# A fifth table-multiplied tile in a product-key memory kernel: head 4's last tile goes through its whole table instead of being gathered

## Chip, cores and metric

The kernel runs on one core of a Trainium2 chip. The metric is the device time of one execution in microseconds (us), smaller being better; the median of three runs is taken. The five engines of the core (TensorE or PE, VectorE or DVE, ScalarE or ACT, GpSimd or POOL, SyncE or SP) run their own instruction queues in order and wait for one another on semaphores.

## What is computed

For each of 16 batches of 512 tokens with 128 features there is a graph layer (layer norm, two products, a mean over neighbours, relu, residual) and then a memory layer with 8 heads. Per head and token, two lists of 128 scores give the 16 best each, the 256 sums give the 16 best pairs, and their softmax weighs 16 rows of keys and values out of a table of 16384 rows. Causal attention over the 512 tokens follows.

```python
q = (x @ Wq).reshape(b, n, HEADS, DIM) * DIM ** (-0.5)
kv_scores, indices = _pk(x, Wq_pk, pk_keys)          # 16 of 16384 rows per head and token
ind = indices + offsets[None, None, :, None]
k = jnp.einsum('bnhk,bnhkd->bnhd', kv_scores, keys_table[ind])
v = jnp.einsum('bnhk,bnhkd->bnhd', kv_scores, values_table[ind])
sim = jnp.einsum('bihd,bjhd->bhij', q, k)
sim = jnp.where(causal, sim, neg)
attn = jax.nn.softmax(sim, axis=-1)
out = jnp.einsum('bhij,bjhd->bhid', attn, v)
return out.transpose(0, 2, 1, 3).reshape(b, n, HEADS * DIM) @ Wo
```

## The kernel before, in words

A batch has 512 tokens, T = 4 tiles of 128. Heads 0 to 6 (GH = 7) are **gathered**: the loop of a batch runs over 28 tiles n (head n // 4, tile n % 4). For each tile GpSimd issues 16 indirect DMAs (L391) that bring 128 rows of 1 KB each into one of three buffers `got`; before them it waits for the row numbers (`rows_ready`) and, since there are three buffers, for the combination that last read this buffer (`combined`). TensorE combines the rows with their weights in 32 instructions into `comb_ps` (L664), ScalarE scales them into `kv`, and attention follows: transposed keys (L544), scores (L548), `prob` transposed (L554), values (L560), the product with Wo (L566). After tiles 1 and 3 of a head TensorE moves the next head's chosen rows and weights onto partitions (`move`, L499), which VectorE has prepared (`one_hot`, `hot_rows`, `sum_rows`, `lift`); VectorE then writes `rows` and `spread` (`take_moved`). At tile 0 of a head TensorE makes the next head's key scores and queries (`front`, L463 and L467) before it combines.

Head 7 is not gathered but **multiplied with its whole table** (the "dense" work). A pass k does this for 2 of the 128 keys of one side and 2 tiles: ScalarE raises four 128x128 exponentials (`raise_`, L790), VectorE compares ranks with counts and multiplies (`weigh`, L1214), TensorE transposes the four results (`turn`, L509), ScalarE copies them out (`take_wideT`, L725), and TensorE multiplies them with four 128x256 pieces of the table, eight instructions in the trace, adding up in `dense_ps` (`multiply`, L523). The buffers `expo`, `wide` and `wideT` are double. There are 64 passes for tiles 0 and 1 and 64 for tiles 2 and 3, 128 a batch. SyncE loads the table in chunks of 8 keys (1 MB) into two buffers `tab`; a load waits for `dense_done` of the chunk that it overwrites, and TensorE waits for `tab_loaded` every 4 passes. Before a half can start, VectorE ranks its scores and builds "hits", which TensorE adds to counts and ranks in `comb_ps` (`add_hits`, L490): four sets a half, eight a batch, at the tiles that `HITS` names.

The passes are laid between the steps of the gathered tiles by hand. `MIDDLE` has a row of five numbers for each of the 28 tiles of batches 0 to 14, `ENDING` for those of the last batch; they say how many passes each engine does after the combination, after the transposed keys, after the scores, before and after the transposed `prob`:

```python
THREE = (1, 0, 1, 1, 0)
FOUR = (1, 0, 1, 1, 1)
FIVE = (1, 1, 1, 1, 1)
SIX = (2, 1, 1, 1, 1)
SEVEN = (2, 1, 1, 2, 1)
```

`MIDDLE` has 16, 18, 20, 19, 19, 18 and 18 passes in its seven heads; `ENDING` 16, 22, 23, 23, 22, 22 and none in the last head. The next batch's graph layer lies at tiles 8 to 20, head 7's attention at tiles 17, 18, 1 and 2 (`OWN`, `LEFT`). In the text a "move" is L499, "fronts" are the operations that write `front_ps`.

Of the kernel before, what the change touches and what calls it, by code (L numbers as in the profile page):

```python
# [8 lines left out]
AX = mybir.AxisListType  # L9

P = 128
# [17 lines left out]

HALF_PASSES = NKEYS // 2  # L30
PASSES = 2 * HALF_PASSES
CHUNK = 4
KEYS = 2 * CHUNK
CHUNKS = PASSES // CHUNK

# [5 lines left out]
SEVEN = (2, 1, 1, 2, 1)  # L41
NONE = (0, 0, 0, 0, 0)
MIDDLE = [
    FIVE, FOUR, FOUR, THREE,
    SIX, FOUR, FIVE, THREE,
    SIX, FIVE, FIVE, FOUR,
    SIX, FIVE, FIVE, THREE,
    SIX, FOUR, FIVE, FOUR,
    SIX, FOUR, FIVE, THREE,
    SIX, FIVE, FOUR, THREE]  # L50
ENDING = [
    FIVE, FOUR, FOUR, THREE,
    SEVEN, FIVE, SIX, FOUR,
    SEVEN, FIVE, SIX, FIVE,
    SEVEN, FIVE, SIX, FIVE,
    SIX, FIVE, SIX, FIVE,
    SEVEN, FIVE, SIX, FOUR,
    NONE, NONE, NONE, NONE]
# [7 lines left out]
PREP = {1: 0, 0: 20}  # L66
HITS = {1: {4: (0, 1), 8: (2, 3)}, 0: {24: (0, 1), 26: (2, 3)}}
# [13 lines left out]
PAIRS = [(0, 2), (2, 2)]  # L81
FIRST_TILES = [(0, 1), (1, 1), (2, 2)]
# [15 lines left out]
def got_no(n):  # L98

    return n % 3 if n < SLOTS - 1 else 1  # L100


def got_back(n):

    return next(d for d in range(1, 6) if got_no((n - d) % SLOTS) == got_no(n))
# [16 lines left out]
def program(nc, x, adj, w_msg, w_upd, bias, wqpk_t, keys_t, wq, table, dense, wo, out):  # L122
# [78 lines left out]
    sim_d = sb("sim_d", [P, T, SIDES * NKEYS])  # L201
# [10 lines left out]
    z_inv = sb("z_inv", [P, T])  # L212
# [3 lines left out]
    rank1 = sb("rank1", [P, T, NKEYS])  # L216
    shift1 = sb("shift1", [P, T, NKEYS])
# [71 lines left out]
    dense_done, kv_d_copied = sem("dense_done"), sem("kv_d_copied")  # L289
    keyT_d_ready, keyT_d_copied = sem("keyT_d_ready"), sem("keyT_d_copied")  # L290
# [25 lines left out]
    def _(sp):  # L316
# [12 lines left out]
        def load_chunk(b, c, first=False):  # L329

            if not (first and c < 2):
                sp.wait_ge(dense_done, b * PASSES + (c - 1) * CHUNK)
            k = (c % (CHUNKS // 2)) * KEYS
# [15 lines left out]
        def batch(b, first=False, last=False):  # L349
# [5 lines left out]
            for c in range(CHUNKS):  # L355
                if c == 5 and not first:
                    store(b - 1)
                load_chunk(b, c, first)
# [6 lines left out]
    def _(pool):  # L365
# [13 lines left out]
        def batch(b, first=False, last=False):  # L379
            for n in range(SLOTS):  # L380
                h, t = n // T, n % T
                slot = b * SLOTS + n
# [3 lines left out]
                if not (first and n < 3):  # L386
                    pool.wait_ge(combined, slot - (got_back(n) - 1))
# [12 lines left out]
    def _(pe):  # L400
# [39 lines left out]
        def front(b, h, first=False, last=False):  # L440

            f = b * GH + h
            if h == 0:
                pe.wait_ge(xnT_copied, b * 2 + 2)
                pe.wait_ge(sim_d_copied, b * 2 + 1)
# [4 lines left out]
            elif h == 2:  # L450
                pe.wait_ge(sim_d_copied, b * 2 + 2)
                if not first:
                    pe.wait_ge(added_d, b * 4)
            elif h == 3:
                pe.wait_ge(q_d_copied, b + 1)
# [984 lines left out]
```

## Time and profile before

| | us |
|---|---|
| median of 3 runs | 9090.88 (9089.48 to 9093.23) |
| the profiled execution's own time | 9084.84 |
| its span, first to last instruction | 9083.0 |
| PE busy | 7878.3 (87%) |
| PEld (weight loads, beside PE) busy | 6137.2 (68%) |
| DVE busy | 7108.3 (78%) |
| ACT busy | 4886.8 (54%) |
| POOL busy | 6820.4 (75%) |
| mean granted TensorE clock | 0.928 of full |

A busy share is an average over the span. GpSimd's issue gaps between gathers are not counted as busy. A granted clock of 1.00 is 2.4 GHz, of 0.50 is 1.2 GHz; the engine has these two levels, and a mean lies between. The ends of matmuls are modelled, so that neighbouring groups overlap.

### The profile page before, as it was taken

What the parts mean: (1) busy time and instruction counts of PE and PEld (TensorE: products, weight loads), DVE (VectorE), ACT (ScalarE), POOL (GpSimd) and SP (SyncE); (2) the same over time, 40 slices, a digit from 0 to 9 for tenths busy, and PEclk for the clock granted to TensorE, in tenths of its full rate; (3) what the DMA queues carried; (4) which work ended last, traced back from release to release, by engine and by line L of the source; (5) the groups of instructions that cost most, each with busy time, mean ns of one, the idle gap of its engine ahead of it and who ended that gap; (6) DMA issues with size and microseconds to landing.
All of it is one profiled execution on the core that took longest, in us unless ns stands there. A gap on an engine that the chain in (4) does not pass through costs nothing.

```text
span 9083.0 us, 179526 instructions
## 1 busy us (share of the span) xinstructions
PE 7878.3 (87%) x51232; PEld 6137.2 (68%) x51232; DVE 7108.3 (78%) x30205; ACT 4886.8 (54%) x14163; POOL 6820.4 (75%) x7177
## 2 busy tenths in 40 slices
PE   5988888888888888888888888898888888889898
PEld 4766667667666766766667666676766766667676
DVE  7787787777878778787787877878778787787875
ACT  3555555555555555555555555464555555555554
POOL 5777777777777777777777777777777777777777
PEclk7999999999999999999999999999999999999998
DMA  4555555555555555555555555555555555555554
GB/s 133 170 171 165 168 168 170 168 167 167 172 165 167 171 166 168 170 167 166 166 172 166 168 169 168 168 171 168 169 166 169 168 166 170 172 162 171 162 179 146
DMA packets 445970, 1516.75 MB, mean 167 GB/s; under 512 B 123760, under 2 KB 141552, under 8 KB 379248
## 3 DMA queue, kind: packets, MB, share of 16 engines
q0 software_dynamic: 344064, 939.98, 33.8%
q1 hardware_dynamic: 100848, 564.37, 17.1%
q8 instruction: 456, 7.47, 0.3%
q14 instruction: 602, 4.93, 0.2%
HBM read 1499.66 MB, written 4.19 MB: 166 GB/s over the span
## 4 chain that ended last, share of the span: by engine, by line
POOL 49%; issue 18%; PE 16%; DVE 15%; ACT 1%; DMA 1%; POOLq 0%; DVEq 0%; SPq 0%; ACTq 0%
POOL got L391 49%; PE dense_ps L523 6%; DVE wide L1214 4%; PE comb_ps L664 3%; DVE hits L1178 2%; DVE chosen L1109 2%; PE wideT_ps L509 2%; DVE onehot L1104 1%; PE front_ps L463 1%; DVE onehot L1097 1%; PE score_ps L499 1%; DMA got<-in_table,rows 1%; DVE lifted L1117 1%; PE score_ps L548 1%; PE front_ps L467 1%
## 5 line engine op out<-in xcount | busy, mean ns | idle before, releaser
L391 POOL DMA_INDIRECT got<-in_table,rows x7168 | 6818.5, 951 | 2245.6 <-issue 2168.4
L523 PE MATMUL dense_ps<-tab,wideT 128*128 128x256 f32 x16384 | 4030.5, 390 | 10.6 <-ACT kv_d L725 9.4
L523 PEld LDWEIGHTS dense_ps<-tab,wideT 128*128 128x128 f32 x16384 | 3053.3, 195 | 669.9 <-issue 265.1
L1214 DVE SCALAR_TENSOR_TENSOR wide<-const_ps,rank,expo 128x128 f32<-128x128 f32 x8192 | 2299.3, 343 | 1357.6 <-PE wideT_ps L509 1039.4
L790 ACT ACTIVATE expo<-sim_d,shift 128x128 f32<-128x128 f32 x8192 | 2598.9, 394 | 128.8 <-DVE wide L1214 127.9
L725 ACT ACTIVATE wideT<-wideT_ps 128x512 f32<-128x512 f32 x2048 | 1212.9, 592 | 676.6 <-PE wideT_ps L509 669.9
L509 PE MATMUL wideT_ps<-ident,wide 128*128 128x128 f32 x8192 | 1255.4, 276 | 265.7 <-ACT wideT L725 243.1
L509 PEld LDWEIGHTS wideT_ps<-ident,wide 128*128 128x128 f32 x8192 | 1023.3, 143 | 534.4 <-issue 286.3
L664 PE MATMUL comb_ps<-got,spread 128*32 128x256 f32 x14336 | 1031.5, 436 | 135.6 <-DMA got<-in_table,rows 107.8
L664 PEld LDWEIGHTS comb_ps<-got,spread 128*32 128x32 f32 x14336 | 469.6, 122 | 587.7 <-issue 245.1
L725 ACT ACTIVATE kv<-comb_ps,wsum 128x256 f32<-128x256 f32 x448 | 210.4, 470 | 909.3 <-PE comb_ps L664 909.1
L499 PE MATMUL score_ps<-group_of,lifted 128*128 128x16 f32 x1792 | 296.9, 300 | 395.2 <-DVE lifted L1117 395.2
L499 PEld LDWEIGHTS score_ps<-group_of,lifted 128*128 128x128 f32 x1792 | 274.3, 234 | 439.2 <-DVE lifted L1117 414.4
L1178 DVE TENSOR_SCALAR hits<-iota_f,top_f_d,put 128x128 bf16<-128x128 f32 x2048 | 555.6, 365 | 0.6 <-DVE count_sb L1200 0.2
L725 ACT ACTIVATE sim<-front_ps 128x512 f32<-128x512 f32 x224 | 133.8, 597 | 669.9 <-PE front_ps L463 666.6
L830 ACT ACTIVATE prob<-neg,neg_max 128x128 f32<-128x128 f32 x448 | 250.9, 560 | 450.9 <-DVE neg_max L1231 450.6
L548 PE MATMUL score_ps<-keyT,qT 128*128 128x512 f32 (+3 forms) x896 | 341.5, 463 | 78.8 <-ACT keyT L725 78.8
L1109 DVE TENSOR_REDUCE chosen<-onehot 128x32 f32<-128x1600 f32 (+1 forms) x225 | 406.1, 1805 | 2.8
L1097 DVE TENSOR_TENSOR onehot<-place,const_ps 128x1600 f32<-128x1600 uint32 (+1 forms) x225 | 406.9, 1808 | 0.0
L1104 DVE TENSOR_TENSOR onehot<-onehot,const_ps 128x1600 f32<-128x1600 f32 (+1 forms) x225 | 405.5, 1802 | 0.1
L463 PE MATMUL front_ps<-w_sim,x2nT 128*128 128x256 f32 x888 | 358.3, 574 | 28.7 <-issue 28.7
L560 PE MATMUL score_ps<-probT,kv 128*128 128x128 f32 x2240 | 335.8, 281 | 53.2 <-ACT probT L725 53.2
(167 smaller groups left out, 7386.0 us busy)
## 6 DMA issues: line engine op xcount, KB each, us to landing
tab<-in_dense SPq DMA_DIRECT2D x512, 1024.0 KB
got<-in_table,rows POOLq DMA_INDIRECT x7168, 2.7
adj_i<-in_adj SPq DMA_DIRECT2D x16, 1024.0 KB
x_in<-in_x SPq DMA_DIRECT2D x16, 256.0 KB, 6.4
out<-fin SPq DMA_DIRECT2D x16, 256.0 KB, 6.0
tab<-in_wqpk_t SPq DMA_DIRECT2D x1, 512.0 KB, 10.5
tab<-in_keys_t SPq DMA_DIRECT2D x1, 512.0 KB, 14.8
wq_sb<-in_wq SPq DMA_DIRECT2D x1, 512.0 KB, 13.5
```

The lines of the kernel that those rows point to most:

```text
L391: pool.indirect_dma_start(out=got[got_no(n)][:, g, :], out_offset=None, in_=table, in_offset=bass.IndirectOffsetOnAxis(ap=rows[:, t * GATH ...
L499: mm = pe.matmul(moved_ps[:, 2 * q + u, :], lifted[:, u, q, :, :].rearrange("p e r -> p (e r)"), group_of[:, :], start=True, stop=True)
L509: mm = pe.transpose(wideT_ps[:, q * P:(q + 1) * P], wide[k % 2][:, q, :], ident[:, :])
L523: mm = pe.matmul(dense_ps[:, v * 2 * D:(v + 1) * 2 * D], wideT[k % 2][:, (2 * u + v) * P:(2 * u + v + 1) * P], tab[(k // CHUNK) % 2][:, (2 ...
L664: mm = pe.matmul(comb_ps[j * BAND:(j + 1) * BAND, 0:2 * D], spread[:, t, g, :], got[got_no(n)][:, g, :], start=(c == 0), stop=(c == PER_BA ...
L725: return act.activation(dst, src, ACT.Copy, scale=scale)
L790: last = act.activation(expo[k % 2][:, 2 * u + v, :], sim_d[:, 2 * half + v, 0:NKEYS], ACT.Exp, bias=shift1[:, 2 * half + v, key:key + 1])
L1097: after(link(dve.tensor_tensor(onehot[:, 0:nt, :, :].rearrange("p t k c -> p (t k) c"), place[:, t0:t0 + nt, :].rearrange("p t k -> p (t k ...
L1104: after(link(dve.tensor_tensor(hot, hot, cand[:, 0:nt, 1, :].unsqueeze(2).broadcast_to([P, nt, TOPK, NCAND]), ALU.mult)))
L1109: link(dve.tensor_reduce(chosen[:, 0:nt, 0, :], onehot[:, 0:nt, :, :], AX.X, ALU.add))
L1178: last = dve.tensor_scalar(hits[g % 2][:, a, :], iota_f[:, :], top_f_d[:, u, side, a:a + 1], put[:, u, side, a:a + 1], ALU.is_equal, ALU.mult)
L1214: last = dve.scalar_tensor_tensor(wide[k % 2][:, 2 * u + v, :], count_ps[:, v, :], rank1[:, 2 * half + v, key:key + 1], expo[k % 2][:, 2 * ...
```

## The change

Tile 3 of head 4 is called `EXTRA_SLOT` (n = 19). It isn't gathered or combined: GpSimd skips it, and a batch has `GSLOTS` = 27 gathered tiles. Instead it has 32 passes of its own (`half` 2) between head 7's two halves. One such pass takes 4 keys for one tile, with the same four exponentials, compares, transposes and products as the others, and its chunk of the table (8 keys of head 4) lasts 2 passes and not 4. The sum goes from `dense_ps` into `kv` (`take_extra`, at tile 16, 17 or 18). A batch has 160 passes and 48 chunks, ten sets of hits, and three preparations of scores, of which the new one starts at tile 0 and that of tiles 2 and 3 of head 7 moves to tiles 6 to 14. The tables of passes are new throughout.

```diff
+EXTRA = 4
+EXTRA_SLOT = EXTRA * T + T - 1
+GSLOTS = SLOTS - 1
+KEYS = 8
 HALF_PASSES = NKEYS // 2
-PASSES = 2 * HALF_PASSES
-CHUNK = 4
+EXTRA_PASSES = NKEYS // 4
+PASSES = 2 * HALF_PASSES + EXTRA_PASSES
+PART = {0: 0, 2: HALF_PASSES, 1: HALF_PASSES + EXTRA_PASSES}
...
+EIGHT = (2, 1, 2, 2, 1)
 MIDDLE = [
-    FIVE, FOUR, FOUR, THREE,
+    EIGHT, SIX, FIVE, FOUR,
...
-PREP = {1: 0, 0: 20}
-HITS = {1: {4: (0, 1), 8: (2, 3)}, 0: {24: (0, 1), 26: (2, 3)}}
+HITS = {2: {4: (0, 1)}, 1: {12: (0, 1), 14: (2, 3)}, 0: {24: (0, 1), 26: (2, 3)}}
...
+def places(k):
+    half, r = part_of(k)
+    if half == 2:
+        return [(j, 4 * r + j, 0) for j in range(4)]
+    return [(2 * u + v, 2 * r + u, v) for u in range(2) for v in range(2)]
+def chunk_of(k):
+    half, r = part_of(k)
+    return ORDER[half] * PART_CHUNKS + r // (2 if half == 2 else 4)
...
             for n in range(SLOTS):
-                h, t = n // T, n % T
-                slot = b * SLOTS + n
+                t = n % T
+                if n == EXTRA_SLOT:
+                    continue
+                slot = gslot(b, n)
                 pool.wait_ge(rows_ready, slot + 1)
...
             if not (first and c < 2):
-                sp.wait_ge(dense_done, b * PASSES + (c - 1) * CHUNK)
+                sp.wait_ge(dense_done, b * PASSES + (chunk_end(c - 2) if c >= 2 else chunk_end(c - 2 + CHUNKS) - PASSES))
...
+        def take_extra(b, n):
+            act.wait_ge(dense_done, b * PASSES + PART[1])
+            act.wait_ge(z_ready, b * 3 + (ORDER[2] + 1))
+            copy(kv[:, T - 1, :], dense_ps[:, 0:2 * D], scale=z_inv[:, T:T + 1]).then_inc(kv_x_copied, 1)
```

The passes of the seven heads are now 25, 22, 25, 21, 25, 24 and 20 in `MIDDLE`, and 25, 24, 27, 22, 28, 27 and 7 in `ENDING`. `move` and `lift` handle one tile instead of two for the second pair of head 4.

The first place is TensorE's queue at tile 3 of head 4 in the loop over the batches (n = 19): `comb_ps` is the combination, `dense_ps` and `wideT_ps` are a pass. Before:

```order
L566 MATMUL probT_ps<-wo_sb,headT 128x128
L596 MATMUL front_ps<-wo_sb,headT_d 128x128
L664 MATMUL comb_ps<-got,spread 32x256 x16
L523 MATMUL dense_ps<-tab,wideT 128x256 x4
L506 REGISTER_ALU
L509 MATMUL wideT_ps<-ident,wide 128x128 x4
L541 REGISTER_ALU
L544 MATMUL probT_ps<-ident,kv 128x128
```

Now:

```order
L647 MATMUL probT_ps<-wo_sb,headT 128x128
L677 MATMUL front_ps<-wo_sb,headT_d 128x128
L603 MATMUL dense_ps<-tab,wideT 128x256 x4
L584 REGISTER_ALU
L587 MATMUL wideT_ps<-ident,wide 128x128 x4
L625 MATMUL probT_ps<-ident,kv 128x128
```

The combination is gone, and the transposed keys read what `take_extra` wrote.

The second place is TensorE's queue at tile 0 of head 0 in the same loop, from the scores to the transposed `prob`. Before:

```order
L548 MATMUL score_ps<-keyT,qT 128x128
L517 ISA
L519 REGISTER_ALU
L523 MATMUL dense_ps<-tab,wideT 128x256 x4
L506 REGISTER_ALU
L509 MATMUL wideT_ps<-ident,wide 128x128 x4
L523 MATMUL dense_ps<-tab,wideT 128x256 x4
L506 REGISTER_ALU
L509 MATMUL wideT_ps<-ident,wide 128x128 x4
L554 MATMUL probT_ps<-ident,prob 128x128
```

Now, up to the fourth pass:

```order
L629 MATMUL score_ps<-keyT,qT 128x128
L603 MATMUL dense_ps<-tab,wideT 128x256 x4
L584 REGISTER_ALU
L587 MATMUL wideT_ps<-ident,wide 128x128 x4
L603 MATMUL dense_ps<-tab,wideT 128x256 x4
L584 REGISTER_ALU
L587 MATMUL wideT_ps<-ident,wide 128x128 x4
L603 MATMUL dense_ps<-tab,wideT 128x256 x4
L584 REGISTER_ALU
L587 MATMUL wideT_ps<-ident,wide 128x128 x4
L603 MATMUL dense_ps<-tab,wideT 128x256 x4
L584 REGISTER_ALU
```

Two passes stood between the scores and the transposed `prob`, and now four do; the tile has eight instead of five.

## Rows read from the trace of the kernel before

**Rows 1.** The page's busy line: us, share of the span, instructions.

```profile
PE 7878.3 (87%) x51232; PEld 6137.2 (68%) x51232; DVE 7108.3 (78%) x30205; ACT 4886.8 (54%) x14163; POOL 6820.4 (75%) x7177
```

**Rows 2.** The page's group of gathers; then GpSimd's waits: us, times, longest.

```profile
L391 POOL DMA_INDIRECT got<-in_table,rows x7168 | 6818.5, 951 | 2245.6 <-issue 2168.4 <-DVE rows L1127 58.1 <-PE comb_ps L664 19.1
...
POOL got L391 <- issue: 2168.4, 7117, 0.3
POOL got L391 <- DVE rows L1127: 58.1, 27, 40.5
POOL got L391 <- PE comb_ps L664: 19.1, 24, 12.1
```

**Rows 3.** Stretches (us): length, busy time (instructions) by engine, TensorE clock, DMA share, GB/s.

```profile
2984.40:3384.60 400.20, 351.00 (x2290) 274.74 (x2291) 310.06 (x1308) 222.86 (x643) 303.00 (x320) 0.94 0.52 169
8608.80:9008.40 399.60, 368.47 (x2440) 295.21 (x2439) 306.47 (x1257) 240.14 (x708) 302.40 (x320) 0.97 0.54 177
...
2909.90:3471.20 561.30, 488.94 (x3197) 381.85 (x3196) 444.16 (x1884) 304.75 (x884) 425.24 (x447) 0.93 0.52 168
```

**Rows 4.** The same two stretches, passes' products (line 523) alone.

```profile
2984.40:3384.60 400.20, 183.51 (x752) 138.84 (x752) 0.94 0.52 169
8608.80:9008.40 399.60, 216.94 (x896) 165.07 (x896) 0.97 0.54 177
```

**Rows 5.** TensorE's waits from 8608.8 to 9008.4: us in total, times, longest.

```profile
PE score_ps L499 <- DVE lifted L1117: 14.3, 9, 2.0
PE probT_ps L566 <- ACT headT L725: 6.6, 18, 0.4
PE wideT_ps L509 <- ACT wideT L725: 5.6, 2, 2.8
```

**Rows 6.** TensorE's waits from 2984.4 to 3384.6.

```profile
PE score_ps L499 <- DVE lifted L1117: 14.7, 10, 3.6
...
PE comb_ps L664 <- DMA got<-in_table,rows: 7.3, 4, 3.2
```

**Rows 7.** Timeline of TensorE: start, duration (us), instruction, count.

```profile
8943.33 1.89 PE L523 MATMUL dense_ps<-tab,wideT 128*128 128x256 f32 x8
...
8945.50 1.89 PE L523 MATMUL dense_ps<-tab,wideT 128*128 128x256 f32 x8
...
8947.67 1.89 PE L523 MATMUL dense_ps<-tab,wideT 128*128 128x256 f32 x8
```

**Rows 8.** A whole batch and the dense stretch: operations on front_ps, then hits (line 490).

```profile
2909.90:3471.20 561.30, 50.10 (x175) 33.45 (x174) 4.92 (x16) 20.17 (x41) 0.93 0.52 168
8608.80:9008.40 399.60, 20.04 (x62) 11.98 (x61) 1.40 (x4) 10.10 (x20) 0.97 0.54 177
...
2909.90:3471.20 561.30, 8.25 (x128) 7.72 (x128) 0.93 0.52 168
8608.80:9008.40 399.60, 3.90 (x64) 3.74 (x64) 0.97 0.54 177
```

**Rows 9.** Groups of combinations: whole span, then from 8608.8 to 9008.4.

```profile
L664 PE MATMUL comb_ps<-got,spread 128*32 128x256 f32 x14336 | 1031.5, 436 | 135.6 <-DMA got<-in_table,rows 107.8 <-DVEq L1202 26.6
...
L664 PE MATMUL comb_ps<-got,spread 128*32 128x256 f32 x640 | 43.7, 419 | 0.3
```

**Rows 10.** Groups of VectorE and ScalarE, whole span: busy, mean ns, idle before.

```profile
L1214 DVE SCALAR_TENSOR_TENSOR wide<-const_ps,rank,expo 128x128 f32<-128x128 f32 x8192 | 2299.3, 343 | 1357.6 <-PE wideT_ps L509 1039.4 <-ACT expo L790 88.6 <-DVE top_i L1046 50.9
L1178 DVE TENSOR_SCALAR hits<-iota_f,top_f_d,put 128x128 bf16<-128x128 f32 x2048 | 555.6, 365 | 0.6 <-DVE count_sb L1200 0.2 <-DVE rank L1197 0.2
L790 ACT ACTIVATE expo<-sim_d,shift 128x128 f32<-128x128 f32 x8192 | 2598.9, 394 | 128.8 <-DVE wide L1214 127.9 <-DVEq L1157 0.2
L725 ACT ACTIVATE wideT<-wideT_ps 128x512 f32<-128x512 f32 x2048 | 1212.9, 592 | 676.6 <-PE wideT_ps L509 669.9 <-PE dense_ps L523 0.6
```

**Rows 11.** Issue of a table chunk; GB/s in 0.25 us slices from 3036 to 3046.

```profile
3037.87 0.33 SPq L334 DMA_DIRECT2D tab<-in_dense  x1
...
GB/s 66 0 0 246 197 82 0 0 246 229 49 164 262 131 393 295 492 360 459 426 492 360 361 328 426 426 279 131 147 262 131 16 33 229 213 66 0 33 213 229
```

More of the change, by code:

```diff
@@ L81, with pair, tiles, tiles_before @@
 PAIRS = [(0, 2), (2, 2)]
+def pair(h, i):
+    return (2, 1) if h == EXTRA and i == 1 else PAIRS[i]
+def tiles(h):
+    return T - 1 if h == EXTRA else T
+def tiles_before(b, h):
+    if h == GH:
+        return (b + 1) * GSLOTS
+    return b * GSLOTS + (h * T - (1 if h > EXTRA else 0))
+def gslot(b, n):
+    return b * GSLOTS + (n - (1 if n > EXTRA_SLOT else 0))
+def part_of(k):
+    half = 0 if k < PART[2] else 2 if k < PART[1] else 1
+    return half, k - PART[half]
+def places(k):
[6 more added lines that the diff above has]
+    return ORDER[half] * PART_CHUNKS + r // (2 if half == 2 else 4)
+def chunk_end(c):
+    return next(k + 1 for k in reversed(range(PASSES)) if chunk_of(k) == c)
+def prep(b, n, last):
+    if n < 6:
+        return 2, b, n
+    if n < 15:
+        return 1, b, n - 6
+    if n >= 20 and not last:
+        return 0, b + 1, n - 20
+    return None, b, -1
+def sets_before(n, last):
+    return 4 + sum(len(g) for half in (2, 1, 0) if not (half == 0 and last)
+                   for m, g in HITS[half].items() if m < n)
 FIRST_TILES = [(0, 1), (1, 1), (2, 2)]
@@ L98, in got_no @@
 def got_no(n):
-    return n % 3 if n < SLOTS - 1 else 1
-def got_back(n):
-    return next(d for d in range(1, 6) if got_no((n - d) % SLOTS) == got_no(n))
+    return (n - (1 if n > EXTRA_SLOT else 0)) % 3
 def dense_tile(b, n, first, last):
@@ L355, in batch @@
             for c in range(CHUNKS):
-                if c == 5 and not first:
+                if c == 6 and not first:
                     store(b - 1)
@@ L473, in front_dense @@
             pe.wait_ge(xnT_copied, b * 2 + 2)
-            for t in (2 * half, 2 * half + 1):
-                last = pe.matmul(front_ps[1][:, (t % 2) * 256:(t % 2 + 1) * 256], x2nT[:, t * P:(t + 1) * P],
-                                 w_sim[:, DENSE * 256:(DENSE + 1) * 256], start=True, stop=True)
+            h = EXTRA if half == 2 else DENSE
+            for i, t in enumerate((T - 1,) if half == 2 else DTILES[half]):
+                last = pe.matmul(front_ps[1][:, i * 256:(i + 1) * 256], x2nT[:, t * P:(t + 1) * P],
+                                 w_sim[:, h * 256:(h + 1) * 256], start=True, stop=True)
             last.then_inc(sim_d_ready, 1)
@@ L931, in batch @@
                     exponent_dense(c, tile)
-                k = passes(b, k, w[3], first, last)
+                k = passes(b, k, w[3], first, last, n)
                 take_probT(slot, t)
@@ L935, in batch @@
                     take_probT_dense(c, tile)
-                k = passes(b, k, w[4], first, last)
+                k = passes(b, k, w[4], first, last, n)
                 take_headT(slot)
@@ L1429 @@
         "table": c(table[:GH * ROWS]),
-        "dense": c(table[DENSE * ROWS:].reshape(NKEYS, NKEYS, 2 * D).transpose(1, 0, 2)),
+        "dense": np.concatenate([table[h * ROWS:(h + 1) * ROWS].reshape(NKEYS, NKEYS, 2 * D).transpose(1, 0, 2)
+                                 for h in (DENSE, EXTRA)], axis=1),
         "wo": c(L0_ffn_Wo),
```

298 lines of the change are left out of this document (157 added, 141 removed).

## The prediction

> **What bounds the kernel now.** I read the page's busy line first, then who waits for whom on GpSimd, then stretches of the loop, and last the waits of TensorE. The busy line puts TensorE at 87% and GpSimd at 75% [rows 1], yet it is GpSimd that sets the time. Its 7168 gathers take 951 ns each and leave only their own issue gap; (6818.5 + 2168.4) / 7168 = 1.254 us per gather, and it waited for others only 58.1 + 19.1 us in 9083 [rows 2]. So 7168 x 1.254 = 8987 us of the span are gathers, 561.7 us for each of the 16 batches, and 96 us are start and tail.
>
> The reader should see next how close TensorE is behind. I compare two stretches of five heads (20 tiles, 320 gathers each). In the middle of a batch they take 400.2 us with 752 / 8 = 94 passes; in the last batch, whose table of passes is denser and which prepares no next batch, 399.6 us with 896 / 8 = 112 passes [rows 3, 4]. (One pass is four transposes and eight matmul instructions on TensorE.) In the first stretch TensorE waits 7.3 us for gathers, so it has a little to spare [rows 6]. In the second it waits for no gather at all: what idles it are its own chains, the results of VectorE for the moves (14.3 us) and ScalarE's copies for the projection (6.6 us) [rows 5]. TensorE works 368.47 of 399.6 us there. **At 22.4 passes a head TensorE needs just what GpSimd needs.** That is the densest stretch the trace has, and the change puts 160 / 7 = 22.9 passes a head into every batch, with less gather time to put them beside.
>
> **What the change removes.** Sixteen gathers a batch: 256 x 1.254 = 321 us of GpSimd. GpSimd alone would then need 6912 x 1.254 = 8668 us, 541.7 us a batch. One combination a batch goes too: 43.7 us for 20 of them is 2.2 us of TensorE [rows 9], with half a move about 2.5 us. VectorE ranks one tile of head 4 less for the gather and one more for the table; I cost that at nothing, covered by its idle fifth [rows 1].
>
> **What it adds.** 32 passes a batch. On TensorE back to back at full clock they start 2.17 us apart (8943.33, 8945.50, 8947.67) [rows 7]: 69.4 us a batch, 1111 us in all, against 1205 us in which TensorE is idle now (9083.0 - 7878.3, [rows 1]). On ScalarE a pass costs (2598.9 + 1212.9) / 2048 = 1.86 us, on VectorE 2299.3 / 2048 = 1.12 us [rows 10]. ScalarE goes from 4887 to about 5840 us and stays hidden. VectorE gets 36 us a batch and two sets of hits (32 x 555.6 / 2048 = 8.7 us) on top of 444.16 [rows 3, 10], near 490 of 590 us: hidden as well, but with less cover in the tiles where hits are built.
>
> **The sum for TensorE, one batch.** I take the dense stretch as the pace, because it has almost the density that every batch will have, and the waits inside it are chains that the change leaves in place.
> - 28 tiles at 399.6 / 20: 559.4 us; they hold 156.8 passes.
> - 3.2 passes more, x 2.17: 6.9 us.
> - What a middle batch has and the dense stretch hasn't (the graph layer, the fronts and all four tiles of head 7): operations on front_ps keep TensorE busy 50.10 us in a whole batch and 20.04 x 1.4 = 28.1 in the dense stretch's measure [rows 8]. The difference is 22.0, at a granted clock of 0.93 against 0.97; at the denser pace I take 19, and 0.6 for the fifth tile's scores.
> - Ten sets of hits at 8.25 / 8 = 1.03 us less the 3.90 x 1.4 that the stretch already holds [rows 8]: 4.8 us.
> - The combination and half move that go: -2.5 us.
> - Waits for the table: one chunk now lasts two passes in the new part and not four. A load issued at 3037.87 is seen as 279 to 492 GB/s from about 3039.5 to 3042.8 (slices 14 to 26 [rows 11]), so it takes some 5 us; two passes back to back last 4.3 us. So a chunk can be late by up to 0.8 us where nothing lies between passes, 13 us over 16 chunks at worst, nothing at best. Most passes have other work between them: I take 1 us.
>
> SyncE issues these 16 loads a batch; behind them in its queue stand the store of the batch before and the next batch's inputs, which nobody waits for within a head, so I cost them at nothing. The DMA engines were 52% busy [rows 3]; 16 MB of table more for 2 MB of gathers less lifts that to some 60%. The last batch has its 160 passes in 25 tiles and I count it as the others.
>
> That is 589 us a batch, where GpSimd would need 541.7. The bound moves to TensorE. 16 x 589 + 96 = 9520 us of span. The profiled execution's own time lies 1.8 us above its span and the median of the three runs 6 us above that, so I forecast **9528**, rounded 9530 us, 4.8% slower. GpSimd's row of waits should show the other side of it: about 16 x 47 = 750 us of waiting for combinations in place of 19.1.
>
> Two terms are open. The granted clock is 0.94 in the middle stretch and 0.97 in the dense one [rows 3]; if the rest went to full clock (half the rate for 6% of 400 us), the stretch loses 12 us and a batch 17. On the other side the middle stretch idles 400.2 - 351.0 = 49.2 us, 7.3 of it for gathers, against 31.1 in the dense one: 10.8 us more, 15 a batch, that tiles with the graph layer, hits and ranks of the next batch may keep. I let the two cancel, and keep 572 and 604 us a batch as ends: 9256 and 9768 us.
>
> **Rivals.** (1) **GpSimd stays the bound and the kernel is faster.** TensorE's idle time takes in the passes, and the end is 541.7 x 16 + 96 + 8 = 8770 us. The comparison of stretches speaks for it: 18 passes more in the same 400 us. It holds if the waits on VectorE and ScalarE shrink when passes lie around them. The point of decision can be worked out: with this sum TensorE's busy time is 368.47 x 1.4 + 6.9 + 19.6 + 4.8 - 2.5 = 545 us a batch, so even the present 561.7 us leaves 17 us of idle, and 541.7 leaves none, while the waits for moves and projections alone were 20.9 x 1.4 = 29 us. Only a much better clock and shorter chains together could do it. A rule of the Trainium skill would choose this rival: "Perfetto Trace Analysis", section "Identifying the Most-Contended Engine", holds that matmul busy time misjudges the headroom, since matmuls are pipelined, and that the busy share of weight loads tells it. By that measure TensorE has room: 295.21 of 399.6 us, 74%, in the dense stretch [rows 3], and the time would be 8770. This trace speaks against the rule: passes 2.17 us apart with no wait between them are the pace of the engine itself [rows 7], whatever share the weight loads have.
>
> (2) **The passes are nearly free, and the time falls a little.** If only the idle that existed beside gathers were filled, at the price that the two stretches show (none), a batch is 561.7 - 6.7 for the gathers no longer waited for (107.8 / 16, [rows 9]) + 2.1 + 0.6 - 2.5 = 555 us, 8990 us in all. Against it: the second stretch had no work on the next batch (the front_ps operations of which a batch has 22 us more [rows 8]), so its passes were not free but exchanged.
>
> (3) **Each pass costs its whole 2.17 us**, on top of the middle batch's idle: 561.7 - 6.7 + 69.4 + 2.1 + 0.6 - 2.5 = 624.6 us, 10098 us in all. The late tables (13 us a batch) or a VectorE that becomes the slower one in the tiles with hits would lead there. It needs the present idle to be incompressible, and the dense stretch shows it isn't.
>
> (4) **The change does not do what it says**: the gathers or the passes would not be those counted. The order of instructions shows both, so I give it nothing.
>
> **Chances.** Forecast with its open terms, 9256 to 9768: 0.75. Between 9109 and 9256, where clock and chains both improve: 0.07. Above 9768 up to rival 3: 0.05. Rival 1: 0.06; rival 2: 0.04. Within 0.2% of 9091, which is about what a measurement of this kernel can tell from no change: 0.03. The range that should hold the time 8 times in 10 is 9230 to 9770. Faster 0.10, same 0.03, slower 0.87.
>
> **What would show it.** In the changed profile GpSimd's gathers should be 6912, still near 1.25 us apart when they run, with many hundreds of us of waiting for comb_ps; TensorE's wait for gathers should be almost gone, its busy share 91 to 93%, its clock 0.95 or more; a batch should take near 589 us, all of the middle batches alike. Waits of dense_ps for a DMA of the table should be small and lie between passes 64 and 96. If GpSimd waits less than 100 us, I am wrong by rival 1; if TensorE's busy share stays at 87% at a longer time, by rival 3, and the waits before wideT_ps or score_ps name the cause.

## The result, and the profile after

The changed kernel takes **10109.77 us** (four runs, 10095.33 to 10130.76) against 9091.05 for the kernel before beside it: a ratio of 1.1122 [1.1102, 1.1142]. I had forecast 9530 with 9230 to 9770. The sign was right, the size less than half of the truth, and the time lies outside the range. The profiled execution took 10130.76 us, its span is 10128.9.

The busy line, the granted clock in slices and the chain that ended last, of the page of the changed kernel:

```profile
PE 8959.0 (88%) x57344; PEld 7125.1 (70%) x57344; DVE 7781.8 (77%) x33101; ACT 5769.5 (57%) x16755; POOL 6572.5 (65%) x6921
...
PEclk8999999999999999999999899999999999999999
...
PE 49%; DVE 40%; issue 5%; ACT 3%; DMA 1%; DVEq 1%; POOL 1%; ACTq 0%; SPq 0%; POOLq 0%
PE dense_ps L603 22%; DVE wide L1311 12%; PE comb_ps L747 7%; PE wideT_ps L587 6%; DVE hits L1272 5%; DVE chosen L1199 4%; DVE onehot L1194 3%; PE front_ps L540 3%; DVE onehot L1187 3%; PE score_ps L577 3%; DVE lifted L1207 1%; PE front_ps L544 1%; DVE neg L1328 1%; DVE sim_rest L1132 1%; DMA tab<-in_dense 1%
```

TensorE did 1081 us more work (8959.0 - 7878.3, [rows 1]) in 1046 us more of span. Its idle time hardly moved: 10128.9 - 8959.0 = 1170 us against 1205. The mean granted clock is 0.940 where it was 0.928; with the two levels that is 2 x 0.060 x 10128.9 = 1215 us at the lower one against 2 x 0.072 x 9083 = 1308. The two lines of the chain are the ones to look at: it is 49% TensorE and 40% VectorE, and GpSimd has 1% of it.

GpSimd's waits, of the changed kernel (us in total, times, longest); before it had 19.1 us for combinations [rows 2]:

```profile
POOL got L467 <- issue: 2251.2, 6761, 12.1
POOL got L467 <- DVE rows L1217: 805.9, 126, 42.8
POOL got L467 <- PE comb_ps L747: 483.1, 25, 32.1
```

TensorE's two longest waits of the kernel before, over its whole span:

```profile
PE score_ps L499 <- DVE lifted L1117: 395.2, 224, 15.1
PE wideT_ps L509 <- ACT wideT L725: 243.1, 131, 4.3
```

And its waits in the changed kernel:

```profile
PE score_ps L577 <- DVE lifted L1207: 396.2, 209, 15.1
PE wideT_ps L587 <- ACT wideT L807: 324.3, 198, 5.5
PE probT_ps L647 <- ACT headT L807: 140.9, 384, 0.4
PE score_ps L629 <- ACT keyT L807: 44.2, 124, 0.5
PE comb_ps L568 <- DVE hits L1272: 41.8, 29, 15.1
PE dense_ps L603 <- DMA tab<-in_dense: 37.6, 28, 2.5
```

The wait before moves (L577) is still about 400 us, though 512 passes more lie around the moves. It comes 209 times, about 13 times a batch, and lasts until VectorE has its one-hot chain (`one_hot`, `hot_rows`, `sum_rows`, `lift`) done. My reading is that a pass more in front of such a wait doesn't shorten it because VectorE has to do its share of that pass too; the run with only TensorE's work added, below, bears this out.

Stretches of the changed kernel: heads 1 to 5 of a middle batch with 117 passes, then of the last batch with 128, and a whole middle batch (length, busy PE, PEld, DVE, ACT, POOL, granted clock, DMA share, GB/s). They answer to [rows 3] (head 0 of `MIDDLE` has 23 passes, not the 25 in the list of the change; heads 1 to 5 are as listed there):

```profile
3328.60:3778.40 449.80, 401.87 (x2562) 319.34 (x2564) 345.58 (x1476) 262.54 (x759) 290.19 (x306) 0.95 0.54 177
9637.00:10070.90 433.90, 405.77 (x2632) 328.90 (x2631) 335.40 (x1399) 272.18 (x802) 284.90 (x300) 0.96 0.57 189
...
3240.00:3868.90 628.90, 559.79 (x3586) 444.81 (x3585) 485.96 (x2067) 360.54 (x1048) 408.99 (x431) 0.94 0.53 174
```

A batch takes 629 us (over the whole span (10128.9 - 96) / 16 = 627.1), not 589. The middle stretch is longer than the last batch's with 11 passes fewer. TensorE's two longest waits in that middle batch (3240.0 to 3868.9):

```profile
PE score_ps L577 <- DVE lifted L1207: 23.5, 13, 3.6
PE wideT_ps L587 <- ACT wideT L807: 20.7, 13, 3.2
```

The chain that ended last, from a middle batch (start us, us, what; xN pieces on end), at the end of head 0 and in head 1:

```profile
3315.95 0.44 PE probT_ps L635 x4
3316.38 1.73 PE dense_ps L603 x8
3318.11 0.45 PE wideT_ps L587 x4
...
3318.91 0.86 DVE wide L1311 x3
3319.77 1.74 DVE chosen L1199
...
3321.60 0.70 DVE lifted L1207
...
3322.35 1.06 PE score_ps L577 x8
3323.41 2.37 PE front_ps L540 x8
...
3334.11 2.04 DVE hits L1272 x8
3336.15 0.77 DVE top L1128 x4
...
3337.98 1.02 DVE wide L1311 x4
3339.00 2.14 DVE hits L1272 x8
...
3343.21 0.20 DVE neg L1328
...
3343.76 0.19 ACT prob L921
3343.95 0.49 ACT wideT L807
...
3344.57 0.52 PE wideT_ps L587 x3
```

Up to 3318.6 it is TensorE that is late. Then VectorE finishes its `wide`, sums the one-hot rows, and TensorE idles until 3322.35. From 3334 to 3341 VectorE builds hits and negates the scores (`neg`) only at 3343.21. ScalarE stands at the exponentials of `prob`, which need them, and its copy of `wideT` comes behind these; TensorE waits 2.9 us for that copy. The two engines take turns as the slower one, and a wait "for ScalarE" can be one for VectorE.

The granted clock around the first of these two waits (columns as above):

```profile
3320.00:3322.00 2.00, 0.30 (x2) 0.10 (x1) 1.90 (x2) 0.00 (x0) 1.64 (x2) 1.00 0.66 217
3325.00:3327.00 2.00, 2.00 (x4) 1.04 (x4) 1.35 (x5) 0.69 (x2) 1.63 (x2) 0.50 0.36 92
```

While TensorE idles, the clock is still 1.00; shortly after, with the engine busy all the time, it is 0.50. So such a wait costs its own length and then something more. Not every drop in this trace follows so plain a wait.

### The profile page after: what moved, and what is told of

Its sections match the earlier page's. It is cut to its first block, busy times and chain, and to the rows that moved or that the text cites. A ratio compares the mean times of both kernels' runs of the same rounds, so it can differ in the third digit from the quotient of the medians.

```text
span 10128.9 us, 201313 instructions
## 1 busy us (share of the span) xinstructions
PE 8959.0 (88%) x57344; PEld 7125.1 (70%) x57344; DVE 7781.8 (77%) x33101; ACT 5769.5 (57%) x16755; POOL 6572.5 (65%) x6921
## 4 chain that ended last, share of the span: by engine, by line
PE 49%; DVE 40%; issue 5%; ACT 3%; DMA 1%; DVEq 1%; POOL 1%; ACTq 0%; SPq 0%; POOLq 0%
PE dense_ps L603 22%; DVE wide L1311 12%; PE comb_ps L747 7%; PE wideT_ps L587 6%; DVE hits L1272 5%; DVE chosen L1199 4%; DVE onehot L1194 3%; PE front_ps L540 3%; DVE onehot L1187 3%; PE score_ps L577 3%; DVE lifted L1207 1%; PE front_ps L544 1%; DVE neg L1328 1%; DVE sim_rest L1132 1%; DMA tab<-in_dense 1%
## 5 line engine op out<-in xcount | busy, mean ns | idle before, releaser
L467 POOL DMA_INDIRECT got<-in_table,rows x6912 | 6570.6, 951 | 3540.2 <-issue 2251.2
L603 PE MATMUL dense_ps<-tab,wideT 128*128 128x256 f32 x20480 | 5026.7, 389 | 46.9 <-DMA tab<-in_dense 37.6
L603 PEld LDWEIGHTS dense_ps<-tab,wideT 128*128 128x128 f32 x20480 | 3816.2, 195 | 782.3 <-issue 254.0
L1311 DVE SCALAR_TENSOR_TENSOR wide<-const_ps,rank,expo 128x128 f32<-128x128 f32 x10240 | 2866.4, 342 | 1670.1 <-PE wideT_ps L587 1370.6
L873 ACT ACTIVATE expo<-sim_d,shift 128x128 f32<-128x128 f32 x10240 | 3246.8, 393 | 135.8 <-DVE wide L1311 133.9
L807 ACT ACTIVATE wideT<-wideT_ps 128x512 f32<-128x512 f32 x2560 | 1517.2, 593 | 1445.9 <-PE wideT_ps L587 1428.1
L587 PE MATMUL wideT_ps<-ident,wide 128*128 128x128 f32 x10240 | 1576.6, 277 | 332.2 <-ACT wideT L807 324.3
L587 PEld LDWEIGHTS wideT_ps<-ident,wide 128*128 128x128 f32 x10240 | 1283.6, 143 | 665.4 <-issue 386.1
L1272 DVE TENSOR_SCALAR hits<-iota_f,top_f_d,put 128x128 bf16<-128x128 f32 x2560 | 694.2, 364 | 0.6 <-DVE z_inv L1284 0.2
L577 PE MATMUL score_ps<-group_of,lifted 128*128 128x16 f32 x1728 | 294.5, 305 | 396.2 <-DVE lifted L1207 396.2
L577 PEld LDWEIGHTS score_ps<-group_of,lifted 128*128 128x128 f32 x1728 | 273.3, 240 | 437.3 <-DVE lifted L1207 412.5
L807 ACT ACTIVATE headT<-score_ps 128x128 f32<-128x128 f32 x448 | 124.0, 277 | 498.2 <-PE score_ps L641 497.7
L1187 DVE TENSOR_TENSOR onehot<-place,const_ps 128x1600 f32<-128x1600 uint32 (+1 forms) x225 | 393.5, 1749 | 0.0
## 6 DMA issues: line engine op xcount, KB each, us to landing
tab<-in_keys_t SPq DMA_DIRECT2D x1, 512.0 KB, 14.7
```

Source lines behind the costliest of these rows:

```text
L467: pool.indirect_dma_start(out=got[got_no(n)][:, g, :], out_offset=None, in_=table, in_offset=bass.IndirectOffsetOnAxis(ap=rows[:, t * GATH ...
L577: mm = pe.matmul(moved_ps[:, 2 * q + u, :], lifted[:, u, q, :, :].rearrange("p e r -> p (e r)"), group_of[:, :], start=True, stop=True)
L587: mm = pe.transpose(wideT_ps[:, q * P:(q + 1) * P], wide[k % 2][:, q, :], ident[:, :])
L603: mm = pe.matmul(dense_ps[:, v * 2 * D:(v + 1) * 2 * D], wideT[k % 2][:, q * P:(q + 1) * P], tab[c % 2][:, key % KEYS, :], start=(r == 0 a ...
L807: return act.activation(dst, src, ACT.Copy, scale=scale)
L873: last = act.activation(expo[k % 2][:, q, :], sim_d[:, t, 0:NKEYS], ACT.Exp, bias=shift1[:, t, key:key + 1])
```

## The experiments

Theories at the outset: **A**, TensorE's queue sets the time and gathers none of it; **B**, gathers still cost. Later ones are about what VectorE has to do with it. All runs are edits of the kernel after or of the kernel before. The unedited kernel before ran beside each of them, in 9080 to 9101 us. Where an interval stands, there were at least four runs; elsewhere one execution was timed. "Less" and "more" are against 10109.77 us, so a difference can be off by some 20 us, as much as the kernel before moved.

**Half of the gathers left out, after.** GpSimd issues 8 of 16 gathers a tile.

```diff
-                for c in range(PER_BAND):
+                for c in range(PER_BAND // 2):
...
-                                           got[got_no(n)][:, g, :], ...
+                                           got[got_no(n)][:, j * PER_BAND + c % 2, :], ...
```

> The changed kernel with 8 of the 16 gathers of each tile left out (TensorE combines the 8 that came twice, so all else is the same work). Theory A: TensorE's queue is the bound now and gathers cost it nothing, so the time stays at 10110 within 30 us. Theory B: gathers still hold it back (late rows, or table chunks that share the DMA engines with them); then the time falls by more than 150 us, and the waits of dense_ps for tab go to zero.

10108.69 us, where the whole takes 10109.77. Half of the gathers cost nothing any more, neither by their number nor by their DMA traffic; theory B fell. TensorE still waited 26.1 us for the table, so most of that wait isn't the gathers' doing.

**The same in the kernel before.**

> The kernel before with 8 of the 16 gathers of each tile left out. It shows what the other engines need for 128 passes a batch when gathers don't bind. Theory A, as my prediction had it (561.7 - 6.7 us a batch): 8980 us, within 40. Then 32 passes really cost (10110 - 8980) / 512 = 2.2 us each. If it is much lower, 8700 or less, the kernel before hid idle time of TensorE behind gathers and a pass costs 2.75 us or more.

8995.58 us, as expected. The chain, the first two of TensorE's waits, and the two stretches of heads 1 to 5 (94 passes in a middle batch, 112 in the last) of this kernel:

```profile
PE 45%; DVE 45%; issue 5%; ACT 4%; DVEq 1%; DMA 0%; ACTq 0%; SPq 0%
```

```profile
PE score_ps L499 <- DVE lifted L1117: 399.2, 224, 15.1
PE wideT_ps L509 <- ACT wideT L725: 249.6, 142, 4.3
```

```profile
2961.10:3354.60 393.50, 351.11 (x2287) 276.05 (x2286) 308.73 (x1308) 222.80 (x643) 152.40 (x161) 0.94 0.36 119
8541.50:8948.50 407.00, 378.18 (x2440) 301.60 (x2439) 304.85 (x1255) 240.05 (x708) 149.17 (x158) 0.94 0.37 122
```

This run is the key to the case. Taking half of the gathers away wins only 1%: behind GpSimd's 561.7 us a batch stood another bound at (8993.8 - 96) / 16 = 556.1. From there the change costs (10109.8 - 8995.6) / 512 = **2.18 us a pass**, the number of [rows 7]. The stretches of this run and of the kernel after spread around it: (449.8 - 393.5) / 23 = 2.45 us a pass in the middle, (433.9 - 407.0) / 16 = 1.68 in the last batch. The dense stretch, with fewer gathers, takes 407.0 us where it took 399.6 [rows 3], at a clock of 0.94 where it had 0.97; why the clock is lower there, no run shows.

**27 gathered tiles in the kernel before**, without the passes that would replace the 28th.

```diff
+                if n == 19:
+                    continue
...
```

> The kernel before with the gathers of head 4's last tile left out and nothing in their place (its combination reads an old buffer): the gift of the change alone. If only gathers bind, 9091 - 321 = 8770. Theory A says TensorE needs 555 us a batch and takes over at once: 8980, and 250 us or more of GpSimd waiting for comb_ps or rows.

8972.99 us, near theory A's 8980: 107 us less (the kernel before took 9080.03 beside it) of the 321 that the gathers measure. GpSimd then waited 182.2 us for `comb_ps` and 93.3 for `rows`. The gift that the change was to bring was only worth a third, even before the passes were paid.

**Passes laid evenly.** Rows of `MIDDLE` that alternate 7, 5, 6, 5 in place of 8, 6, 5, 4 and the like.

```diff
-    EIGHT, SIX, FIVE, FOUR,
+    SEVEN, FIVE, SIX, FIVE,
...
```

> The changed kernel with another MIDDLE: 160 passes laid 7, 5, 6, 5 over the four tiles of nearly every head, as the dense last batch of the kernel before has them (7, 5, 6, 4), in place of rows such as 6, 7, 6, 3. Theory P (placement): a pass on tile 1 beyond five costs 2 us, one on tile 0 or tile 3 about 1 us, so a batch falls by 15 to 25 us and the time to 9720 to 9880. Theory A: only the number of passes counts; 10110 within 50.

10015.56 us, 1.1032 [1.1013, 1.1050]: 94 us less, more than theory A allows and short of the range of the theory of placement. The waits for the table fell from 37.6 to 13.2 us, those before moves rose to 457.2. So part of what a pass costs is its place: laid evenly it is (10015.6 - 8995.6) / 512 = 1.99 us and not 2.18.

**Fillers before the moves.** Twenty small bf16 products into a spare part of `score_ps` before TensorE waits for `lifted`.

```diff
+            for _ in range(20):
+                pe.matmul(score_ps[:, 384:512], ident_b[:, :], ident_b[:, :], start=True, stop=True)
```

> The changed kernel with 20 products of the bf16 identity with itself, into an unused part of score_ps, before TensorE's wait for `lifted` in every move (224 moves; without them TensorE idles there 1.2 to 3 us and the granted clock drops to 0.5 right after). Theory C: the low clock is set off by these waits and costs what its busy time shows (1053 us of busy time at 0.5, so up to 526 us). Then the clock rises from 0.94 to 0.97 or more and the time falls by 150 to 350 us. Rival: the drops come from other gaps, or the fillers delay the move; then the time stays or rises, by up to 224 x 0.4 us = 90.

9940.63 us, 1.0948 [1.0925, 1.0971]: 169 us less, for work that computes nothing. The clock, and the same two waits, of this kernel:

```profile
core 0: 9923.2 us, clock 0.971
```

```profile
PE wideT_ps L589 <- ACT wideT L809: 373.1, 211, 5.5
PE score_ps L579 <- DVE lifted L1209: 171.3, 152, 11.6
```

The time and the clock are in the range that was expected. The fillers sit where TensorE idled (396.2 to 171.3 us), and time at the lower level falls from 1215 to 2 x 0.029 x 9923.2 = 576 us. So part of what a wait cost was the clock behind it.

**The second part of the hits later**, behind VectorE's negation in that tile.

```diff
-                hit_part(1)
...
+                hit_part(1)
```

> The changed kernel with VectorE's second quarter of the hits moved behind `negate` in the five tiles that have hits. There TensorE waits 2.7 to 3.2 us at wideT_ps for ScalarE, which stands at the exponentials of `prob` until VectorE has negated the scores. Theory D (VectorE is late there): each quarter is 2.2 us, so 2 us x 5 tiles x 15 batches = 150 us are saved, 100 to 250 with the clock. Theory A (TensorE's work alone): within 30 us of 10110.

10105.41 us, 1.1127 [1.1109, 1.1146], the same as the kernel after; nothing of theory D's 100 to 250 us came. TensorE's wait for the copy of `wideT` fell from 324.3 to 179.5 us and one for `wide` itself came in its place; the work was still in VectorE's way:

```profile
PE wideT_ps L587 <- ACT wideT L807: 179.5, 172, 3.6
PE probT_ps L647 <- ACT headT L807: 140.9, 384, 0.4
PE wideT_ps L587 <- DVE wide L1311: 136.5, 76, 2.4
```

**Half of the compares left out.** VectorE does two of the four of a pass.

```diff
-            for q, key, v in places(k):
+            for q, key, v in places(k)[0:2]:
...
```

> The changed kernel with two of the four compares of every pass left out on VectorE (it keeps the other pieces at zero, all engines else do the same work): VectorE loses 0.56 us a pass, 1430 us in all. Theory A (TensorE's queue bounds, VectorE matters only in the tiles with hits): down by less than 250 us. Theory V (VectorE is a second bound all along): down by 500 us or more.

9394.71 us, 715 less, clock 0.972. VectorE was busy 6482.4 us instead of 7781.8, so one us of compares was worth 715 / 1299 = 0.55. Theory A fell here: TensorE's queue doesn't bound by itself, VectorE is a second bound.

**A quarter of the hits built.**

```diff
-            for a in range(part * 4, part * 4 + 4):
+            for a in range(part * 4 + 3, part * 4 + 4):
...
```

> The changed kernel with 4 of the 16 hits of every set built, the others zero: 120 of 160 instructions a batch left out on VectorE, 520 us in all, TensorE's work unchanged. Theory D: all of the 3 us waits in the tiles with hits go and the clock drops with them: 5 x (3 + 1) x 16 = 320 us less, between 200 and 450. Theory A: less than 100 us.

9752.33 us, 357 less for 482 us of VectorE, 0.74 for one and in theory D's range. The wait for `wideT` fell to 130.9 us, that before moves stayed at 394.3.

**Most of the next batch's work left out**: on VectorE its normalisation, its graph layer and the ranking and hits of head 7's first half, on TensorE a part of the same.

```diff
-        def gnn_hu(b):
+        def gnn_hu(b, few=False):
...
-                for t in (2 * i, 2 * i + 1):
+                for t in ((2 * i,) if few else (2 * i, 2 * i + 1)):
...
-                    gnn_in(b + 1)
+                    dve.wait_ge(x_loaded, (b + 1) * 16 + 16)
...
```

> The changed kernel with most of the next batch's work left out of the middle batches: on VectorE its whole graph layer, layer norms, and the ranking and hits of head 7's first half; on TensorE 14 of 16 neighbour products, half of the other graph products, 60 of 64 products of those hits. By my sum this work costs what TensorE is busy with it, (59.9 + 32.2 + 21.0) / 16 + 4 x 1.03 = 11 us a batch: the time falls by 170 us. Theory N (it also sets VectorE back, TensorE waits and its clock falls, which is why the last batch, that has no such work, looked so dense): 35 us in heads 1 to 5 and 12 in the rest, 700 us less, between 550 and 850.

9696.43 us, 413 less, between the two expectations. Over the 15 batches that prepare another it is 27.6 us each, for (8959.0 - 8744.1) / 15 = 14.3 us of TensorE and (7781.8 - 7241.3) / 15 = 36.0 of VectorE. The wait for the copy of `wideT` fell from 324.3 to 158.7 us.

**Even plan and fillers together**, the two edits above in one kernel.

> The changed kernel with the even plan (95 us less alone) and the fillers before the moves (170 us less alone). If both act on different waits they add up: 9840 to 9860. If the even plan only moves idle time to the waits before the moves (457 us there now), the fillers bring more: 9780. Not below 9700 by any theory here.

9872.33 us, 1.0844 [1.0826, 1.0862]. The two nearly add up (237 us less, of 94 + 169 = 263), and this is the best version of the changed kernel that leaves nothing out; it is 8.4% behind the kernel before.

**The fillers in the kernel before.**

> The kernel before with the same fillers. Theory A: GpSimd bounds it, so what the clock gives TensorE is hidden: within 20 us of the kernel before, while its granted clock rises from 0.93 to 0.96. Rival: TensorE is so near behind GpSimd that single late combinations matter; then 30 to 60 us less.

9107.17 us, 1.0007 [0.9998, 1.0017], with the clock at 0.959 instead of 0.928, as theory A had it. There the better clock is hidden behind GpSimd: TensorE's wait before moves falls to 156.8 us, and its wait for gathers grows from 107.8 [rows 9] to 270.4.

**One of four products left out**: TensorE multiplies only three quarters of the pieces of a pass.

```diff
-            for q, key, v in places(k):
+            for q, key, v in [p for p in places(k) if p[0] != 2 or p[1] == NKEYS - 1 or p[1] % NKEYS == NKEYS - 2]:
```

> The changed kernel with one of the four products of nearly every pass left out on TensorE (a quarter of 5026.7 us busy, some 1200 us of its queue). If TensorE's queue alone bounds: 8900, near the 8770 at which GpSimd takes over. If TensorE and VectorE bound in turn, as leaving out 1430 us of VectorE (715 us less) suggests: about half, 9400 to 9600.

9935.06 us. The products fell from 5026.7 to 3977.0 us busy and the time by only 175, so both expectations missed (8900, and 9400 to 9600). This speaks against TensorE's queue as *the* bound. The clock fell to 0.912, TensorE's idle time rose from 1170 to 9933.2 - 8192.0 = 1741 us; the line of the chain by engine, and the first two waits:

```profile
DVE 46%; PE 37%; ACT 7%; issue 7%; DMA 2%; DVEq 1%; POOL 1%; ACTq 0%; SPq 0%; POOLq 0%
```

```profile
PE wideT_ps L587 <- ACT wideT L807: 566.5, 277, 5.2
PE score_ps L577 <- DVE lifted L1207: 531.5, 194, 15.1
```

**One product of a pass twice**, the counterpart.

```diff
-            for q, key, v in places(k):
+            for q, key, v in [p for p in places(k) for _ in range(2 if p[0] == 1 else 1)]:
```

> The changed kernel with one product of every pass done twice on TensorE: some 0.48 us a pass more, 1230 us of its queue in all, no other engine changed. Theory K (the engines stand about even, so cutting one hands over to the other at once while adding to one costs in full): 11100 to 11400. Theory W (TensorE has slack most of the time): 10110 + 175 to + 500.

10387.26 us: 277 more for 6029.5 - 5026.7 = 1003 us more of products. Busy line and chain of this kernel:

```profile
PE 9640.9 (93%) x62464; PEld 7892.6 (76%) x62464; DVE 7794.3 (75%) x33101; ACT 5770.6 (56%) x16755; POOL 6561.8 (63%) x6921
...
PE 57%; DVE 33%; issue 4%; ACT 3%; DMA 1%; DVEq 1%; ACTq 0%; SPq 0%
```

Theory K, a kink at the kernel's own load, fell; theory W held. A microsecond of TensorE's products is worth 0.17 to 0.28 in either direction, if VectorE and the copies get no work with it. The rest is paid by shorter waits (396.2 to 156.0 us before moves, 324.3 to 160.6 for `wideT`; all idle time 10385.4 - 9640.9 = 744.5 us) and a clock of 0.979, which leaves 2 x 0.021 x 10385.4 = 436 us at the lower level.

**Half of the compares and a quarter of the products left out**, the two edits above in one kernel.

> The changed kernel with both cuts: half of VectorE's compares and a quarter of TensorE's products. Alone they save 715 and 175 us. Theory K: together more than their sum of 890, down to 8900 or less, where GpSimd's 8770 stops it. Theory of independent costs: 9220 within 60.

9077.92 us, 1032 less, where the single cuts sum to 715 + 175 = 890. With VectorE lighter, the products are worth 317 us and not 175: each engine hides a part of the other. Theory K had this sign, but not its size (8900 or less), and the costs aren't independent (9220).

**Half of the exponentials left out.** ScalarE raises two of four.

```diff
-            for q, key, v in places(k):
+            for q, key, v in places(k)[0:2]:
...
```

> The changed kernel with two of the four exponentials of every pass left out on ScalarE (half of 3246.8 us, 1620 us). ScalarE is 57% busy and nearly always waited for after it has itself waited. If it is no part of the loop: less than 60 us. If its copies and exponentials lie between TensorE and VectorE: 200 us or more.

10122.42 us, no change, for 1450 us less of ScalarE (5769.5 to 4319.9). ScalarE's raising is not on the chain, as predicted; what waits "for ScalarE's copy of wideT" waits for what the copy waits for. This run also answers a doubt about the half of the compares: there TensorE multiplied zeros in two of four pieces, and here it does the same and gains nothing, so the 715 us are VectorE's time and not the zeros'.

**One-hot products for one tile of each pair.** VectorE leaves out half of the two long multiplications and of the sum before moves.

```diff
-                    one_hot(t0, nt)
+                    one_hot(t0, 1)
...
-                    hot_rows(nt)
+                    hot_rows(1)
...
-                    sum_rows(nt)
+                    sum_rows(1)
```

> The changed kernel with the one-hot products and sums of each pair of tiles done for one tile (the other keeps old row numbers): VectorE loses 3 x 0.9 us for 208 pairs, some 560 us. These stand right ahead of the moves that TensorE waits for. Theory P2 (place on the chain decides): 75% or more of it comes back, over 420 us, the wait before the moves falls from 396 to under 150 us. If a microsecond of VectorE is worth the same everywhere, as in its compares (half): 280 us.

9534.81 us, 575 less for 7781.8 - 7271.3 = 510 us of VectorE: 1.13 for one, the dearest microsecond of this kernel, and theory P2 held. The chain and the waits of this kernel:

```profile
PE 62%; DVE 25%; issue 5%; ACT 5%; DMA 1%; DVEq 0%; POOL 0%; ACTq 0%; SPq 0%; POOLq 0%
```

```profile
PE wideT_ps L587 <- ACT wideT L807: 352.6, 197, 5.5
PE probT_ps L647 <- ACT headT L807: 140.6, 384, 0.4
PE score_ps L577 <- DVE lifted L1207: 64.6, 35, 15.1
```

The wait before moves fell by 332 us; the time at the lower clock fell too, from 1215 to 2 x 0.032 x 9533 = 610 us.

| left out or added | busy us of its engine | time | per us |
|---|---|---|---|
| one-hot chain, VectorE | -510 | -575 | 1.13 |
| hits, VectorE | -482 | -357 | 0.74 |
| compares, VectorE | -1299 | -715 | 0.55 |
| products added, TensorE | +1003 | +277 | 0.28 |
| products left out, TensorE | -1050 | -175 | 0.17 |
| exponentials, ScalarE | -1450 | +13 | 0 |
| gathers, GpSimd | -3281 | -1 | 0 |

## Why the prediction was wrong

**The gathers' side was right.** GpSimd alone needs 541.7 us a batch and now waits: 805.9 + 483.1 = 1289 us for others. I expected about 750 for combinations alone; with the batch 38 us longer the wait is longer too, and most of it shows as waiting for `rows`, which hang on the moves. TensorE's wait for gathers fell from 107.8 [rows 9] to 1.2 us. The sign that I had named for rival 3 came too: TensorE's busy share stayed at 88% where I expected 91 to 93%, and the two longest waits stand before `score_ps` and `wideT_ps`.

**The price of a pass came out, but not for my reason.** I had 69.4 us a batch for 32 passes, 2.17 each; the run with half the gathers gives 2.18. My 2.17 was TensorE's own pace. Where TensorE alone got or lost products, a microsecond of them was worth 0.17 to 0.28, an even plan makes the pass 1.99, and half of VectorE's compares are worth 715 us. That all this comes to 2.18 is in part luck. Taken back to 128 passes, my sum is 589 - 69.4 (passes) - 2.1 (two sets of hits) + 2.5 (combination) - 1 (table) = 519 us. The run gave 556.1. **Nearly the whole error of 38 us a batch is in this base**, and it was there before the change: the prediction's step "I take the dense stretch as the pace" set it 37 us too low.

Where the 40 us of a middle batch lie on TensorE can be read from its trace, 629 us against my sum. The engine was busy 559.79 us, where the sum had 545, at a clock of 0.94 and not the dense stretch's 0.97. It idled 628.90 - 559.79 = 69.1 us, where the sum had 44. The largest piece of these 25 us is the wait for the copy of `wideT`, 20.7 us against 5.6 x 1.4 = 7.8 [rows 5]; the wait before moves gives 23.5 against 20.0. The first is the wait that shrank when hits or the next batch's work were left out.

Three things are in that step. *The pace itself*: with half of the gathers gone the dense stretch takes 407.0 us and not 399.6, 10 us when scaled by 1.4. *The next batch's work* went in by TensorE's busy time: 22.0 us, taken as 19. Where most of it was left out, the same way of counting gives 14.3 us of TensorE, and the time fell 27.6 us, with 36.0 us of VectorE gone as well. *Eight of the 28 tiles* were not in the stretch at all, those of heads 0 and 6, with two of the hits' tiles and few passes. In the kernel before with half the gathers they take 556.1 - 393.5 = 162.6 us; my base leaves them 519 - (399.6 - 18 x 2.17 + at most 24.4) = at least 134. The dense stretch scaled by 1.4 couldn't show them. How the 37 us divide among the three isn't settled, since they overlap.

**VectorE hidden: wrong.** Its busy time I had nearly right (485.96 us in the batch above, "near 490"). But a share of 77% hid nothing where VectorE's long operations stand in one piece and TensorE waits for them: 40% of the chain is VectorE, and its one-hot chain is paid in full (1.13). A row that could have warned me stood in the profile before: TensorE's wait for `lifted`, 14.3 us in 400 with 112 passes [rows 5] and 14.7 with 94 [rows 6], did not depend on the passes. I did keep it, as one of the "chains that the change leaves in place". What I missed is that it names VectorE as an engine on the path, whose 36 us a batch for the passes I then costed at nothing.

**ScalarE hidden: right** for its exponentials, by the run without half of them.

**The clock: wrong.** I expected 0.95 or more from a denser TensorE. It came to 0.940: TensorE's idle time had stayed (1170 us against 1205), and the time at the lower level with it (1215 against 1308). Where an edit shortened the waits, the clock rose: fillers 0.971, lighter one-hot chain 0.968, fewer compares 0.972.

**The table:** 37.6 us in 28 waits, 2.4 a batch where I took 1; the longest is 2.5 us, where my worst case for one chunk was 0.8. They lie where I expected them, nearly all before passes 94 and 96. The even plan leaves 13.2.

**The rivals.** Rival 3 gave 624.6 us a batch and 10098 in all, and the truth is 627.1 and 10110: the number came true by its premise that idle is incompressible, with VectorE as the cause that it named second. Its base of 555 us is what the run with half the gathers measured, 556.1. That it is within 12 us is in part luck, since the placement of the passes alone is worth 94. I dismissed it by one sentence, "the dense stretch shows it isn't". The stretch showed passes exchanged for the next batch's work, as I had written against rival 2 myself. Rival 1, and the rule of the Trainium skill beside it ("Perfetto Trace Analysis", "Identifying the Most-Contended Engine"), were wrong on the time. On TensorE alone the rule has a point: weight loads at 70% say that there was room, and the run with a product twice found it, at 0.28 us for one. My argument against it, that passes 2.17 us apart are the engine's pace, didn't settle that. But room on one engine was not room in the loop.

**No better version.** The best changed kernel that leaves nothing out needs 9872 us. Even with nothing added, leaving the 28th tile's gathers out wins 107 us, which is what three passes a batch cost (3 x 16 x 2.18 = 105); 32 passes can't pay on this chain. Even with half of the one-hot chain gone it takes 9535 us, so halving that chain wouldn't be enough.

What stays open: how much of a pass's 2.18 us is TensorE's work and how much VectorE's (both cuts of a part are cheaper than the whole pass); how the 575 us of the one-hot run divide between shorter waits and clock; and what sets the granted clock. With products left out it fell to 0.912 while TensorE's idle time rose to 1741 us; which of the two brings the other isn't shown.

## What to carry to other kernels

Before you take load off the engine that sets the time, take that load away for nothing and read the time: here half of the gathers gone won 1%, and that one run gives the base on which the replacement is then paid. A dense stretch is only a pace for the others if every engine has the same work there; scale none to tiles that it doesn't hold. Where the chain of waits alternates between two engines, a microsecond's price follows from its place and not from the busy share, from 0 to 1.13 in this kernel. A wait that keeps its length between a thin and a dense stretch isn't covered by more of the same work: here the wait before moves was 395.2 us before the change and 396.2 after it.

## What was unexpected of the hardware

Work that computes nothing made the kernel faster: 20 small products before each move, in a wait, gave 169 us and lifted the mean granted clock from 0.940 to 0.971. One product of four done twice (1003 us busy) cost only 277 us with the clock at 0.979, and one of four left out (1050 us) won only 175 with the clock at 0.912. TensorE's idle time and the time at the lower clock both moved against the edit (744.5 and 436 us in the first case; 1741 and 2 x 0.088 x 9933.2 = 1748 in the second), and so an edit of its work moved the time by much less than its own length.
